# Quaternion attention: the first group's stacks placed by products, keys ahead of queries in token halves, projections as three products of rounded parts

## The reference

```python
x = x + 0.5 * _L1_ffn_ref(_layernorm(x, axis=-1), L1_ffn_gate_query, ...)
x = x + _L1_attn_ref(_layernorm(x, axis=-1), L1_attn_qW, L1_attn_qb, ...)
x = x + 0.5 * _L1_ffn_ref(_layernorm(x, axis=-1), L1_ffn_gate_query, ...)

def _L1_attn_ref(x, qW, qb, kW, kb, vW, vb, oW, ob, J):   # 16 heads of 16
    q = quat_norm(quat_linear(x, qW, qb))
    k = quat_norm(quat_linear(x, kW, kb))
    v = quat_linear(x, vW, vb)
    scores = jnp.einsum('bthd,bshd->bhts', q_, k_) * scale
    scores = scores + jnp.mean(jnp.sin(J[:T])) * 0.1
    attn = jax.nn.softmax(scores, axis=-1)
    out = jnp.einsum('bhts,bshd->bthd', attn, v_).reshape(B, T, D)
    return quat_linear(out, oW, ob)
```

## Time and profile before

| | |
|---|---|
| median of 3 runs | 3194.71 us (3189.52 to 3195.48) |
| the profiled execution | 3197.65 us, its span 3195.9 |
| TensorE busy | 2813.0 us, 88% of the span, granted clock 0.942 of 2.4 GHz |
| VectorE / ScalarE / GpSimd busy | 1801.0 / 1638.5 / 621.8 us |
| first expert stage with Sinkhorn gates | about 1835 to 2192 |
| quaternion attention | about 2192 to 2910, its loop from 2249 |
| shares of the chain that ended last | TensorE 68%, VectorE 11%, GpSimd 7%, ScalarE 5%, issue 4%, DMA 3% |

### The profile page before, as it was taken

The page is one execution under the profiler, slowest core; times in us unless marked ns, Lnnn a source line. Parts: engine busy times, 40 slices in busy tenths (PEclk is TensorE's granted clock), DMA queues, the critical chain, the costliest instruction groups (busy, mean ns, idle before and its releaser), DMA issues.

```text
span 3195.9 us, 52651 instructions
## 1 busy us (share of the span) xinstructions
PE 2813.0 (88%) x21319; PEld 2155.1 (67%) x21319; DVE 1801.0 (56%) x3682; ACT 1638.5 (51%) x2510; POOL 621.8 (19%) x555
## 2 busy tenths in 40 slices
PE   6898999997999879989999926996899999994898
PEld 4677999995666567779999815894233333332898
DVE  5554555547777665545555485785424445335786
ACT  3433555543444344334555423762687777892565
POOL 0036022121000000541121254442000000001343
PEclk9999999998999989999999967998899999996899
DMA  3224243332000021333342434673542423313575
GB/s 128 87 78 129 77 102 86 83 79 67 2 2 2 22 41 43 111 107 96 80 93 73 118 101 119 166 198 76 151 101 42 130 40 107 65 34 113 152 198 133
DMA packets 241795, 290.34 MB, mean 91 GB/s; under 512 B 31300, under 2 KB 218876, under 8 KB 241552
## 3 DMA queue, kind: packets, MB, share of 16 engines
q1 hardware_dynamic: 202624, 226.24, 24.4%
q0 software_dynamic: 34848, 56.28, 8.6%
q10 hardware_dynamic: 4080, 4.46, 0.5%
HBM read 204.72 MB, written 89.50 MB: 92 GB/s over the span
## 4 chain that ended last, share of the span: by engine, by line
PE 68%; DVE 11%; POOL 7%; ACT 5%; issue 4%; DMA 3%; POOLq 1%; SPq 1%; ACTq 0%; DVEq 0%
PE PS L2736 16%; PE PS L159 13%; PE PS L160 12%; PE PS L161 12%; PE PS L995 9%; POOL xe_scratch L788 4%; POOL ZR L208 1%; DVE SM L176 1%; ACT FW L506 1%; PE PS L468 1%; PE PS L2118 1%; POOLq L3063 1%; DVE FW L589 1%; ACT Z L555 1%; PE PS L2808 1%
## 5 line engine op out<-in xcount | busy, mean ns | idle before, releaser
L2851 ACT ACTIVATE P<-PS 128x1024 f32<-128x1024 f32 x512 | 487.4, 1035 | 116.5 <-PE PS L2736 113.8
L159 PE MATMUL PS<-FH,FW 128*128 128x366 f32 (+1 forms) x1408 | 512.6, 364 | 26.3 <-DVE FW L589 13.5
L160 PE MATMUL PS<-FH,FW 128*128 128x366 f32 (+1 forms) x1408 | 502.6, 357 | 0.0
L161 PE MATMUL PS<-FH,FW 128*128 128x366 f32 (+1 forms) x1408 | 499.6, 355 | 0.0
L500 ACT ACTIVATE FHH<-PROD 128x366 fp32r<-128x366 f32 (+1 forms) x352 | 195.3, 555 | 486.5 <-DVE PROD L581 486.5
L159 PE MATMUL PS<-FW,FHH 128*122 128x256 f32 (+1 forms) x1184 | 339.2, 287 | 1.5 <-DVE FHH L584 1.5
L160 PE MATMUL PS<-FW,FHH 128*122 128x256 f32 (+1 forms) x1184 | 335.3, 283 | 0.0
L161 PE MATMUL PS<-FW,FHH 128*122 128x256 f32 (+1 forms) x1184 | 334.3, 282 | 0.0
L581 DVE TENSOR_TENSOR PROD<-SIL,PS 128x366 f32<-128x366 f32 (+1 forms) x352 | 206.8, 587 | 225.4 <-PE PS L161 214.9
L584 DVE TENSOR_TENSOR FHH<-PROD,FHH 128x366 fp32r<-128x366 f32 (+1 forms) x352 | 209.8, 596 | 218.7 <-ACT FHH L500 218.7
L159 PEld LDWEIGHTS PS<-FH,FW 128*128 128x128 f32 x1408 | 268.4, 191 | 55.0 <-DVE FW L589 14.7
(11 more groups left out here) (401 smaller groups left out, 5340.5 us busy)
## 6 DMA issues: line engine op xcount, KB each, us to landing
WS<-L_ffn_w_dram SPq DMA_DIRECT2D x256, 256.0 KB
WST<-L_ffn_W_dram SPq DMA_DIRECT2D x168, 256.0 KB
S<-parts_scratch SPq DMA_DIRECT2D x60, 384.0 KB, 8.2
parts_scratch<-PT SPq DMA_DIRECT2D x32, 512.0 KB, 3.6
Z<-xe_scratch POOLq DMA_DIRECT2D x14, 777.8 KB, 8.5
WST<-L_ffn_W1s_dram SPq DMA_DIRECT2D x40, 256.0 KB
WST<-L_ffn_W3s_dram SPq DMA_DIRECT2D x40, 256.0 KB
WST<-L_ffn_W2s_dram SPq DMA_DIRECT2D x40, 256.0 KB
```

The lines of the kernel that those rows point to most:

```text
L159: e.matmul(o, lh, rh, start=start, stop=False, skip_group_check=True)
L160: e.matmul(o, ll, rh, start=False, stop=False, skip_group_check=True)
L161: return e.matmul(o, lh, rl, start=False, stop=stop, skip_group_check=True)
L2851: e.activation(self.PR[K % 3][:, 2 * jj:2 * jj + 2, :].rearrange("p a b -> p (a b)"), c.pair(2 * ((2 * K + jj) % 3)), ACT.Exp, scale=0.25) ...
```

## The change

The edits fall in five groups.

1. **Scatter and reload.** `YE` is signalled by halves (`yev` twice) and each half's scatters have a counter of their own (`sc0`, `sc1`); the bias product of a half of `dn` stands right behind that half's products. The reload of batch 0 (`xget` 0) waits for `sc0` alone; the other three stand behind the meeting point, at the head of the attention's list.
2. **Products of rounded parts.** `Consts1` gets an item `split` in step 17 (VectorE: three roundings of a 128 x 512 weight into WH, three subtractions into WR); `ht` now writes HB rounded and its low part (HL0 in batch 0, PT of the keys in the others); `pj` is 6 products of float32r by `mm3`, `vv` is 12 of 256 columns. `fo` stays as it was.
3. **First group's stacks.** `sta` takes the place of `direct`: with the 0/1 matrices EB (`eb`, written on VectorE) two products put the rounded and the low part of 32 rows into all 128 rows of a stack, for each of queries and keys, two head pairs and two token halves. The evacuation adds the constant rows, so `rows` fills two stacks and not four.
4. **Order of batch 0.** `start` replaces `prep(0)`: statistics and normalisation in two halves, keys ahead of queries, every step of the first channel block in token halves; ScalarE takes the rounding of HB, six evacuations of projections and part of those of the placed stacks. The queries' second half, three V steps and the second channel block are a queue `rest` that has first call on the turns from K = 0.
5. **Order of batches 1 to 3.** All four V steps stand ahead of the keys' parts, both blocks of which follow one another.

The diff, cut to its core:

```diff
-        return seq + ([("end", n)] if self.final else [("xget", n, b) for b in range(4)])
+        return seq + [("end", n) if self.final else ("xget", n, 0)]
...
+            if jp == 3:
+                w.wait_ge(*p.at(f"b2_{e_ % 2}", ("b2", n, e_)))
...
-            if e_ >= 2:
-                w.wait_ge(*p.at("sc", ("sc", n, e_ - 2)))
             for bb in range(2):
-                ins = e.tensor_scalar(self.YE[e_ % 2][:, bb, :], yb[:, 256 * bb:256 * bb + 256],
-                                      self.GG[:, bb, e_:e_ + 1], None, ALU.mult)
-            ins.then_inc(*p.one("yev"))
+                if e_ >= 2:
+                    w.wait_ge(*p.at(f"sc{bb}", ("sc", n, e_ - 2)))
+                e.tensor_scalar(self.YE[e_ % 2][:, bb, :], yb[:, 256 * bb:256 * bb + 256],
+                                self.GG[:, bb, e_:e_ + 1], None, ALU.mult).then_inc(*p.one("yev"))
 
...
             for bb in range(2):
+                w.wait_ge(*p.at("yev", ("ye", n, e_), 1 - bb))
+                if e_:
+                    w.wait_ge(*p.at(f"sc{bb}", ("sc", n, e_ - 1)))
                 e.indirect_dma_start(
                     out=self.target, out_offset=bass.IndirectOffsetOnAxis(
                         ap=self.IDG.bitcast(U32)[:, bb, e_:e_ + 1], axis=0),
...
-            w.wait_ge(*p.at("sc", ("sc", n, 15)))
+            w.wait_ge(*p.at(f"sc{it[2] // 2}", ("sc", n, 15)))
...
-                for s in range(2):
-                    dst = self.ST[x][s][:, :, :].rearrange("p j (a t) -> p (j a) t", t=128)
-                    e.activation(dst, ones, ACT.Copy, scale=self.BV if x else 1.0).then_inc(*p.one("cr"))
+                dst = self.ST[x][1][:, :, :].rearrange("p j (a t) -> p (j a) t", t=128)
+                e.activation(dst, ones, ACT.Copy, scale=self.BV if x else 1.0).then_inc(*p.one("cr"))
...
+        elif k == "split":
+
+            self.ready(w, "qk", "vo")
+            for nm in "qkv":
+                ins = e.tensor_copy(self.WH[nm][:, :, :], self.W[nm][:, :, :])
+            ins.then_inc(*p.one("dv"))
+            w.wait_ge(*p.mine())
+            for nm in "qkv":
+                ins = e.tensor_tensor(self.low(nm)[:, :, :], self.W[nm][:, :, :], self.WH[nm][:, :, :].bitcast(F32), ALU.subtract)
+            ins.then_inc(*p.one("cs"))
...
+    def start(self):
+
+        n = self.call
+        seq = []
+        for h in range(2):
+            seq += [("stats", n, "p", 0, 4 * h + i) for i in range(4)] + [("root", n, "p", 0, h), ("zz", n, 0, h)]
+        hts = lambda h: [("ht", n, 0, h, cc) for cc in range(2)]
+        parts = lambda x, h: [(k, n, 0, x, 0, h) for k in ("p1", "p2", "p3")]
+        pj = lambda x, h, cc: ("pj", n, 0, x, h, cc)
+        seq += [("xb", n, 0)] + hts(0) + [pj(1, 0, 0), pj(1, 0, 1), ("sq", n, 0, 1, 0)] + hts(1)
+        seq += [pj(1, 1, 0), ("nn", n, 0, 1, 0), pj(1, 1, 1), ("sq", n, 0, 1, 1), pj(0, 0, 0)] + parts(1, 0)
+        seq += [pj(0, 0, 1), ("sq", n, 0, 0, 0), ("nn", n, 0, 1, 1), ("vv", n, 0, 0)] + parts(1, 1)
+        seq += [("nn", n, 0, 0, 0)] + [("sta", n, 1, jj, h) for h in range(2) for jj in range(2)] + [("put", n, 1)]
+        seq += parts(0, 0) + [("sta", n, 0, jj, 0) for jj in range(2)]
+        rest = Jobs()
+        rest.add(0, pj(0, 1, 0))
+        rest.add(1, pj(0, 1, 1), ("sq", n, 0, 0, 1))
+        rest.add(1, ("vv", n, 0, 1))
+        rest.add(1, ("nn", n, 0, 0, 1), *parts(0, 1))
+        rest.add(1, ("vv", n, 0, 2))
+        rest.add(1, ("sta", n, 0, 0, 1), ("sta", n, 0, 1, 1), ("put", n, 0), ("stk", n, 1))
+        rest.add(1, ("vv", n, 0, 3))
+        for x in range(2):
+            rest.add(1, *[(k, n, 0, x, 1) for k in ("p1", "p2", "p3")])
+        return seq, rest
 
     def prep(self, b):
...
+        values(0)
         norm(1, 1)
-        if b:
-            values(1)
-            parts((1, 0))
-            values(2)
-            parts((1, 1))
-            values(3)
-        else:
-            parts((0, 0), (1, 0))
-            q.add(0, ("stk", n, 0), ("put", n, 0), ("put", n, 1))
-            parts((0, 1), (1, 1))
-            q.add(0, ("stk", n, 1))
-            for i in range(4):
-                values(i)
...
-            for q in (fin, ahead, sinking):
+            for q in (rest, fin, ahead, sinking):
...
-                ins = mm(self.pb(it), W[:, q, 128 * cc:128 * cc + 128], self.HB[:, q, 512 * h:512 * h + 512],
-                         q == 0, q == 1)
+                ins = c.mm3(e, self.pb(it), self.k.WH[nm][:, q, cs], self.k.low(nm)[:, q, cs], self.HB[:, q, hs],
+                            self.low(b)[:, q, hs], q == 0, q == 1)
             ins.then_inc(*p.one("pp"))
...
+        elif k == "sta":
+
+            x, jj, h = it[2:]
+            rs, hs = slice(32 * jj, 32 * jj + 32), slice(512 * h, 512 * h + 512)
+            half = ("p2", n, 0, x, 0, h)
+            w.wait_ge(*p.at("eb", ("eb", n)))
+            w.wait_ge(*p.at(self.copier(half), half))
+            w.wait_ge(*p.at("prv", ("p3", n, 0, x, 0, h)))
+            mm(self.pb(it), self.EB[rs, 2 * x, :], self.PT[x][rs, 0, hs], True, False)
+            mm(self.pb(it), self.EB[rs, 2 * x + 1, :], self.QLR[x][rs, 0, hs], False,
+               True).then_inc(*p.one("pp"))
...
+        elif k == "ht" and it[2] == 0:
+            w.wait_ge(*p.at("pp", it))
+            e.activation(self.HB[:, it[4], 512 * it[3]:512 * it[3] + 512], self.pb(it), ACT.Copy).then_inc(*p.one("ha"))
+        elif k == "pj" and self.by(it) == "ha":
+            b, x, h, cc = it[2:]
+            w.wait_ge(*p.at("pp", it))
+            self.k.ready(w, "bi")
+            e.activation(self.QL[x][:, cc, 512 * h:512 * h + 512], self.pb(it), ACT.Identity,
+                         bias=self.k.BI[x][:, cc:cc + 1]).then_inc(*p.one("ha"))
+        elif k == "sta" and self.by(it) == "ha":
+            x, jj, h = it[2:]
+            w.wait_ge(*p.at("pp", it))
+            self.k.ready(w, "bv")
+            e.activation(self.k.ST[x][0][:, jj, 512 * h:512 * h + 512], self.pb(it), ACT.Identity,
+                         bias=self.k.RB[x]).then_inc(*p.one("ha"))
         elif k == "nn":
...
-        elif k == "p2" and it[2] == 0:
+        elif k == "p2" and self.copier(it) == "pra":
             self.part_copy(e, w, it)
-        elif k == "stk" and it[2] == 0:
-            self.direct(e, w, 1)
...
             if b:
                 w.wait_ge(*p.at("pp", ("vv", n, b - 1, 3)))
-            e.tensor_copy(self.HB[:, cc, 512 * h:512 * h + 512], self.pb(it)).then_inc(*p.one("fv"))
-        elif k == "pj":
+                e.tensor_copy(self.HB[:, cc, hs], self.pb(it)).then_inc(*p.one("dv"))
+                self.stored(w, b - 1, 1, cc)
+                w.wait_ge(*p.mine())
+            else:
+                w.wait_ge(*p.at("ha", it))
...
-    def direct(self, e, w, x):
-
-        p, n = self.c.p, self.call
-        by = ("p3", n, 0, x, 0)
-        self.k.ready(w, "rows")
-        for bl, part in enumerate(self.PARTS[x]):
-            w.wait_ge(*(p.at("prv", by) if part else p.at(self.copier(by), ("p2", *by[1:]))))
-            src = self.QL[x][:, 0, :] if part else self.PT[x][:, 0, :].bitcast(F32)
-            for j in range(4):
-                row = 64 * (j % 2) + bl
-                e.dma_start(self.k.ST[x][0][row:row + 46:3, j // 2, :].bitcast(F32),
-                            src[16 * j:16 * j + 16]).then_inc(*p.dma(f"st{x}0"))
-
```

252 lines of the change are left out of this document (165 added, 87 removed), and 2 rows, old and new, of the table COUNTS.

## The result

| | before | changed |
|---|---|---|
| median of 9 runs, us | 3194.71 | 3207.90 |
| lowest and highest | 3189.52 to 3199.23 | 3201.08 to 3216.63 |
| ratio to the kernel before, 95% interval | | 1.0043 (1.0031 to 1.0056) |
| profiled execution and its span | 3197.65, 3195.9 | 3207.95, 3206.1 |

A forecast was written before the change was run, and what follows sets the result against it. TensorE, busy 88% of the span, was taken as the bound, with one dip between second expert stage and attention. Terms summed to -26.9, so 3170.8 for an execution like the profiled one, median 3167.8; range 3159 to 3178.

The forecast's parts named there:

- A: End of second expert stage and reload of X: split scatter starts the attention's statistics earlier, -2.8 us (-1.5 to -3.5).
- B: From X to the attention's first score product: reordered preparation takes 44 us where it took 57.2, -13.2 (-9 to -15).
- Its sign against it: Preparation before the first score product: a wait for HL or the squares over 3 us, counted at 2, would show B wrong.
- C: First attention turns of batch 0: projections, V products and placings moved behind the first score product cost +5.5 (+3.6 to +8).
- D: Attention loop, batches 1 to 3: products of rounded parts shorten 24 projections and 12 V steps, -18.0; lower end -9.
- E: VectorE in the attention loop: second operations per transposed block and the keys' parts in one block cost +1.5 (0 to +5).
- F: Second expert stage: new roundings and subtractions of constants on VectorE, fewer stacks filled by ScalarE, +0.5 (-2 to +3).
- Rival 3: Attention loop: small TensorE gaps in shorter turns bring half clock; with 80 us more of it, 3208; chance 0.03.
- Rival 4: Split scatter or placing products come later than the DMAs did, the new chain crossing engines; B only -3, 3178; chance 0.09.
- Rival 1: Attention loop gives back little, VectorE's queue or the single bank pacing shorter turns; D -7, E +3, 3180; chance 0.16.

The follow-up runs named there:

- e3: Changed kernel with EB's writes moved on VectorE behind the first half's low parts: 1.0014 of the kernel before; last YE to statistics 10.8, was 16.2.
- e5: Changed kernel with the keys' parts of batches 1 to 3 in turns of their own: 1.0038 of the kernel before; loop 648.3, was 654.7.
- e13: Changed kernel as it is, run again as control on the chip of the repeated plain-products run: 1.0041 of the kernel before; loop 655.2.
- e1: Changed kernel with both bias products of an expert behind both token halves again: 0.9981 of the kernel before; period 13.31, was 13.70.
- e2: Kernel before with only the bias products moved between the token halves: 1.0033 of the kernel before; period 13.71, was 13.31.
- e4: Changed kernel with plain float32 products in projections and V of batches 1 to 3: 1.0111 of the kernel before; loop 666.1, was 654.7.
- e8: Changed kernel with the edits of e1, e3 and e5, and batch 0's second channel halves' parts two turns later: 0.9971 of the kernel before.
- e9: Changed kernel with batch 0's second channel halves' parts behind the next batch's root, 12th and 14th turn: 1.0031 of the kernel before.
- e12: The kernel of e9 with GpSimd's additions for batch 1 cut to one column: one execution, no ratio; loop 658.3.

## Why the prediction was wrong, step by step

**A, the end of the expert stage: statistics forecast 9.7 after the last YE, measured 16.2.** The split scatter did what I counted: SP's loads start 3.86 after the first scatter. Two steps failed. I took the meeting point for SP's alone, because the earlier trace rows names SP as what VectorE waited for; GpSimd's drain had ended 2.6 ahead of it and was the next bound. And the writes of EB were counted at 2.5 and as fitting in beside the load of X. They took 6.2, on the path (e3). The 0.2 for each was right for ten of the twelve copies, 0.18; what the count had at nothing is VectorE beside GpSimd's memsets of V, 3.5 for the other two.

**B, to the first score product: forecast 44.0, measured 44.2.** The chain by operation lengths held, gain 13.0. Its sign against it did fire: TensorE waited 5.7 for HL. That is the second half's statistics ahead of the low parts, which the sum had, under another name.

**C, behind the first score product: forecast +5.5 (my own terms make 23.9 + 2 - 20.0 = 5.9), measured +15.9.** From the first score product to the point at which TensorE is done with ten score and eight value steps it is 20.0 before and 35.9 now (2243.18 to 2279.1). I had 23.9 + 2. The turns themselves took 4.4 more: the first two 4.0 and 3.2 where I had 2.1 each, at a granted clock of 0.68 over the first ten, the sixth 3.9, since TensorE waits for the copies of the placed stacks, and each V turn 0.2 more. The rest, 5.6, is one stop that I didn't have: OC's copy behind the parts on VectorE, 4.64, and the value products behind it, 1.93 for 1.0. I wrote of such a queue for batches 1 to 3 only, and for batch 0 costed TensorE alone. Seen by exponentials the loss looks smaller for a while: 14.1 at exponential 24, 5.4 at 40, since the next batch's preparation now comes in later turns, and 12.6 at 88, when it has caught up; by then D has given back 3.8.

**D, products of rounded parts: forecast -18.0, measured -11.4 and -10.8.** The mechanism was right and the size off by 0.2 a turn: a projection saves 0.33, not 0.51, a V step 0.31. The mis-sized term is the difference 1.91 - 1.4. My 1.4 was six times a spacing read inside a long row of such products, and the 1.91 was the whole group from its start to the next row's, with 0.2 at its edges that the new group has as well.

**E, VectorE in the loop: forecast +1.5, measured about +7.** 3.7 in each of two batches, 6.4 of it given back by e5. I named the queue, the block's 6.3 us and its waiters OC and the sinks' copies, and took 2 as the worst for each of three blocks. Behind a block of 6.24 that starts as the step ahead ends, the wait can be 6.24 less what TensorE has to do, and 3.7 it was.

**F, the constants: forecast +0.5, measured within the scatter.** Over the two periods around the constants it is 38.6 before and 39.3 now, less 0.8 for the bias products; the second execution of the changed kernel (e13) has 36.9.

**The missing term, +11.6.** The diff moves two plain products between products of rounded parts. The prediction doesn't mention them: I read the move as a part of the split of YE, which adds no instruction, and gave it no price. The block was in the trace of the kernel before: 1.06 long for two products of 256 columns, with 0.21 ahead of it and 0.22 behind its successor in place of 0.12. Read and asked why, it would have given this term.

Sum: the terms were to give -26.9 in all and gave, on the traces, +3.7 for A, -13.0, +15.9, -11.4 and +7.4, and 11.6 for the bias products is 14.2. Against it stand the start (-1.9) and the stretch behind the last exponential (-2.7: its last sixteen products took 3.7 for 6.2, at a granted clock of 1.00 where it was 0.60 before); that makes 9.6 of the span's 10.2. It is a tally, not a proof: C, D and E make 11.9 of the loop's 13.2, and the loop alone moved by 3 between two executions with the same turns.

**The rivals.** Rival 3 had the time, 3208, by luck and not by its mechanism: TensorE in the side turns is at a granted clock of 1.00. The half clock costs in the first turns of batch 0 and behind TensorE's stops, not in every turn. Rival 4's doubt, that the new chain would be held up, did not come true before the first score. Rival 1 (VectorE's queue paces shorter turns) was the nearest to what happened to D and E, with too small a price.

## What to carry to other kernels

Count the places at which a row of like products on TensorE is interrupted, not the products alone: here the same two bias products, put between the others in two places and not in one, cost 0.39 us more. And compare like with like: a group timed from its start to the next row's start holds its edges, a spacing read inside a row does not, and that took 0.2 off the forecast saving of every group in the loop. When a wait goes, list every engine's arrival at that point, the drains with them, and not only the one that came last. And before work is moved out of a preparation into a loop, add up the other engines' queues in those turns: VectorE had 16.8 us of work (5.4 + 6.2 + 4.5 + 0.7) in ten turns of 1.66, and whichever piece stood first, someone waited for the one behind.

## What the runs showed of the chip

- Breaking into a row of like products costs TensorE time in which it counts as busy: 0.39 us for one more break by a bias product of one row, at full clock, the same in all undisturbed periods of e1 and e2. In the loop 0.2 stands around a projection between value and score products, whether it is plain (before, e4) or rounded (changed), so there it is not the kind of product that costs.
- GpSimd's drain after an indirect scatter lasts 5.3 beyond the scatter's instruction (2183.82 to 2189.12 before, 2186.99 to 2192.28 in the changed kernel, and 5.3 in e1, e3 and e8), while the scatter has landed 3.8 to 3.9 after its start.
- VectorE and GpSimd slow each other down. Beside GpSimd's additions, VectorE's rounding took 1.11 for 0.69 and its subtraction 1.64 for 1.23 (e9, e12), and the eight additions 10.53, where they took 6.41 beside less. The Trainium skill (SBUF — State Buffer, SBUF: two separate sides) has the two share a pair of ports as an exclusive lock held for a whole instruction; the trace agrees that they collide, with 0.4 to 0.5 us for an operation here.
- The loss can be many times the operation: two roundings of 32x32 elements, 0.18 each when alone, took 1.87 and 1.98 beside GpSimd's memsets of 2.21 and 1.93 and ended 0.04 behind them, as for a lock that the other holds to its end. Small operations don't get by cheaply, then; what counts is how long the other engine's instruction is.
